# Two graph layers on one core: gather offsets read from resident tables, block numbers loaded quad by quad

## The chip, the core and the metric

The kernel runs on one core of one Trainium2 chip, in one launch. The metric is the device time of that launch in microseconds. An engine is named as the profile names it: PE (TensorE, with PEld for its weight loads), DVE (VectorE), ACT (ScalarE), POOL (GpSimd) and SP (SyncE, which issues DMAs here). Each has its own instruction queue, and semaphores order the queues against each other.

## The reference

Two attention layers over one graph of 6250 nodes and 106250 edges (50000 pairs in both directions and a loop at each node), the edges sorted by destination. Width 128; the first layer has 8 heads, the second 4. Shortened:

```python
# layer 0
Q, K, V = x @ Wq, x @ Wk, x @ Wv                       # [n, 8, 16]
q_dst = Q[dst] + rel_q[type2]
k_src = K[src] + rel_k[type2] + time_emb @ Wt + bt
v_src = V[src] + rel_v[type2]
euclid = sum(q_dst * k_src) / sqrt(16) * decay          # decay: a small MLP of edge time and type
hyp    = -beta * norm(m[src] - m[dst]) * decay          # m: x mapped into the ball
logits = alpha * euclid + (1 - alpha) * hyp
ex     = exp(logits - segment_max(logits, dst)[dst])
agg    = segment_sum(v_src * ex / denom[dst], dst)
x = layernorm(x + block(x, agg))                        # Wo, two norms, an FFN with gelu
# layer 1
logits = sum(leaky_relu(xs[src] + xd[dst] + edge_emb[type8], 0.2) * att)
agg    = segment_sum(xs[src] * softmax_by_dst(logits), dst)
x = layernorm(x + film_norm(x, agg))
```

## The kernel before

`front` prepares: node tables in DRAM, index tables, the decay of each edge. `edges0` is the first pass over the edges (first layer), then `join_tiles` and `nodes0` finish that layer; `edges1` is the second pass, then `join_tiles` and `nodes1`. The change touches `edges0` and `edges1` alone.

The sorted edges are cut into 831 tiles of 128. The nodes are cut into 53 blocks of 120. A *step* is one tile against one block, so that a tile whose destinations cross a border has two steps; the steps are padded to 896. Four steps are a *quad*, and 221 quads are worked in each pass, one after the other, all written out (`whole(emit)`). Each engine runs its own list `emit(None, c)` for c = 0, 1, ...

**POOL** gathers the rows of the source nodes. `gather(i, c)` issues four indirect DMAs for quad c, each of 128 rows with 128 offsets, one a partition, into a ring of 12 quads in the first pass (`RQ0`) and 16 in the second (`RQ`). Before the four it waits for `sums`: PE must be done with the quad that held this place of the ring. In the kernel before it also waits, once in a group of quads (4 in the first pass, 8 in the second), for `idx_in`. The offsets for all steps lie in one resident table, `k.index0` in the first pass (128 x 896 integers) and `index1` in the second (brought in by a DMA at its start). ACT copies the 16 or 32 columns of one group from it into a small buffer `idx` (three buffers, or two), and the gather reads its offsets from there. ACT's copy itself waits until the rows of an older group have landed (`index`, L1217 and L1936).

**PE** forms, for each quad of the first pass, the time term (L1298), differences and query products by an identity and a transposed one-hot matmul (L1306, L1308), and seven to eight quads later the sums per destination (L1320).

**DVE** does the rest of the first pass in the order of `emit` (L1120): the key addition L1146 (waits for the rows of the quad), the product L1151 (waits for PE's points), the reduction L1156, the transposed one-hot L1117, the one-hot comparison L1164 for the quad 7 back, the scaling of values L1180, and between these four additions `add(0)` to `add(3)` (L1135). Each addition takes one step's result, two more quads back (a = c - 9), and adds it to the block of the accumulator whose number stands in the table `tile_block`. That number must be in a register of DVE's queue before the instruction is issued. `load_steps` (L944) brings numbers there: one load of up to sixteen. Once in four quads there is extra work: L1169 and L1183 in one quad, L1174, L1188, L1195 and L1199 in the next.

Before the change, DVE loads the numbers of four quads at the head of a quad:

```python
if live(i, a) and (a % 4 == 3 or a == 0):
    count["blocks"] = load_steps(nc, k, ET.DVE, 1, nth0(i, a, QS), 4 if a % 4 == 3 else 3)
```

The quad before has ended with a wait for its last addition (L1201) and a count of the semaphore `added` (L1202).

**ACT** copies the sums out of PSUM (L1252), squares differences (L1260) and issues DMAs; **SP** issues the other loads.

The second pass has the same order of things with fewer operations: L1867, L1872, L1876, L1883, L1886, four additions L1896 and the one-hot L1854 on DVE. Its block numbers are loaded by the same helper between L1886 and the additions, those of four quads at a time (of one quad the first time); that is not changed.

Of the kernel before, what the change touches and what calls it, by code (L numbers as in the profile page):

```python
# [20 lines left out]
I32 = mybir.dt.int32  # L21
# [3 lines left out]
ET = mybir.EngineType  # L25

P = 128
# [933 lines left out]
def edges0(nc, k):  # L961
# [7 lines left out]
    with ExitStack() as ctx:  # L969
# [6 lines left out]
        feat = [sb(f"feat{u}", [P, P]) for u in range(6)]  # L976
        idx = [sb(f"idx{u}", [P, GS], I32) for u in range(3)]
        oht = [sb(f"oht{u}", [P, QS * P]) for u in range(3)]
# [17 lines left out]

        weights_in, ready, idx_in = sem("weights_in"), sem("ready"), sem("idx_in")
        node_in, group_in, bound_out = ([sem(f"{m}{u}") for u in range(3)] for m in ("node_in", "group_in", "bound_out"))
# [10 lines left out]
        def live(i, c):  # L1009
            return i is not None or 0 <= c < sz.quads  # L1010
# [13 lines left out]
        with nc.Block() as block:  # L1024
# [60 lines left out]
            @block.gpsimd  # L1085
            def _(pl):
                def gather(i, c):
                    if c % LQ0 == 0:
                        pl.wait_ge(idx_in, group(i, c, 1, 1))
                    if i is not None or c >= RQ0:  # L1090
                        pl.wait_ge(sums, nth0(i, c - RQ0 + 1, 2))
                    apart(pl, k.passed)
                    for t in range(QS):
                        nc.gpsimd.indirect_dma_start(  # L1094
                            rows[:, c % RQ0 * QS + t, 0:3 * D], None, k.d_table0,
                            bass.IndirectOffsetOnAxis(ap=idx[c // LQ0 % 3][:, c % LQ0 * QS + t:c % LQ0 * QS + t + 1], axis=0))\
                            .then_inc(rows_in[c % RQ0], 16)

                for c in range(sz.quads):
                    gather(None, c)  # L1100

            @block.vector
            def _(dve):
# [16 lines left out]
                def emit(i, c):  # L1120
# [3 lines left out]
                    key = rows[:, r:r + QS, 0:D]  # L1124
                    if live(i, a) and (a % 4 == 3 or a == 0):
                        count["blocks"] = load_steps(nc, k, ET.DVE, 1, nth0(i, a, QS), 4 if a % 4 == 3 else 3)

                    def add(t):
                        if not live(i, a):
                            return  # L1130
                        if t == 0:
                            dve.wait_ge(evicted, nth0(i, a + 1, 2))
                        to = acc[:, bass.ds(count["blocks"][((a - 3) % 4 if a >= 3 else a) * QS + t], 1), :]
                        dve.wait_ge(vec, count["added"])
                        v.did(V.tensor_tensor(to, to, bound[a // BQ % 3][0:BN, a % BQ * QS + t, :].unsqueeze(1), ALU.add))  # L1135
                        count["added"] = v.base + v.n
# [24 lines left out]
                    if live(i, w):  # L1161
                        if i is not None or w >= 2:
                            dve.wait_ge(sums, nth0(i, w - 1, 2))
                        V.tensor_tensor(oh[w % 2][:, :, :], bc(k.iota[:, 0:R_LAST + 1], 1, QS),  # L1164
                                        bc(k.code[:, bass.ds(nth0(i, w, QS), QS)], 2, R_LAST + 1), ALU.is_equal)
                    if leveling:
                        u = m // LQ0 % 3
                        dve.wait_ge(rooted, group(i, m, 1, 1))
                        v.did(V.tensor_tensor(far[:, :, :], bc(k.heads[:, 1, :], 2, GS), bc(dist[:, :], 1, H0), ALU.mult))  # L1169
# [30 lines left out]
                    if live(i, a):  # L1200
                        dve.wait_ge(vec, count["added"])  # L1201
                        dve.sem_inc(added, 1)  # L1202
                    count["base"] += v.n

# [9 lines left out]
            def _(act):  # L1214
                A = nc.scalar

                def index(i, c):  # L1217
                    if i is not None or c >= 3 * LQ0:
                        b = c - 2 * LQ0 - 1
                        act.wait_ge(rows_in[b % RQ0], slot(i, b, RQ0, 16 * QS))  # L1220
                    A.copy(idx[c // LQ0 % 3][:, :], k.index0[:, bass.ds(nth0(i, c, QS), GS)]).then_inc(idx_in, 1)

# [13 lines left out]
                def emit(i, c):  # L1236
                    w, m1 = c - LAG0 - 1, c - 3 - LQ0
                    if c % LQ0 == 1 and live(i, c - 1 + 2 * LQ0):
                        index(i, c - 1 + 2 * LQ0)
                    if c % LQ0 == 3 and live(i, m1):  # L1240
# [36 lines left out]

                for g in range(2):
                    index(None, g * LQ0)
                for c in range(5):  # L1280
# [459 lines left out]
def edges1(nc, k):  # L1740
# [5 lines left out]
    with ExitStack() as ctx:  # L1746
# [8 lines left out]
        att = sb("att", [P, D])  # L1755
        idx = [sb(f"idx{u}", [P, LQ * QS], I32) for u in range(2)]
        oht = [sb(f"oht{u}", [P, QS * P]) for u in range(4)]
# [13 lines left out]
        att_in, index_in = sem("att_in"), sem("index_in")  # L1771
        idx_in, node_in = sem("idx_in"), [sem(f"node_in{u}") for u in range(2)]
        gate_in = [sem(f"gate_in{u}") for u in range(2)]
# [15 lines left out]
        with nc.Block() as block:  # L1789
# [29 lines left out]
            @block.gpsimd  # L1819
            def _(pl):  # L1820
                def gather(i, c):
                    if c % LQ == 0:
                        pl.wait_ge(idx_in, c // LQ + 1 if i is None else i * 2 + (c // LQ + 1))
                    if i is not None or c >= RQ:
                        pl.wait_ge(sums, nth(i, c - RQ + 1, 2))
                    apart(pl, k.passed)
                    for t in range(QS):
                        r = c % RQ * QS + t
                        nc.gpsimd.indirect_dma_start(  # L1829
                            rows[:, r, :], None, k.d_table1,  # L1830
                            bass.IndirectOffsetOnAxis(ap=idx[c // LQ % 2][:, c % LQ * QS + t:c % LQ * QS + t + 1], axis=0))\
                            .then_inc(rows_in[c % RQ], 16)

                for c in range(sz.quads):
                    gather(None, c)
# [97 lines left out]
            def _(act):  # L1933
                A = nc.scalar

                def index(i, c):  # L1936
                    u = c // LQ % 2
                    if i is not None or c >= 2 * LQ:
                        b = c - LQ - 1
                        act.wait_ge(rows_in[b % RQ], 16 * QS * (b // RQ + 1) if i is None else i * (16 * QS) + 16 * QS * (b // RQ + 1))  # L1940
                    A.copy(idx[u][:, :], index1[:, bass.ds(nth(i, c, QS), LQ * QS)]).then_inc(idx_in, 1)  # L1941

                def emit(i, c):
                    w, m = c - LAG, c - LQ
                    if c % LQ == 2 and live(i, c - 2 + LQ):
                        index(i, c - 2 + LQ)
                    if c % LQ == 1 and live(i, c - 1 - LQ):
# [25 lines left out]

                act.wait_ge(index_in, 16)
                index(None, 0)
                whole(emit)
# [506 lines left out]
```

## Time and profile before

| what | us |
|---|---|
| the three timed runs | 3217.82, 3219.7, 3222.8 |
| their median | 3219.7 |
| span of the profiled execution, first to last instruction | 3217.7 |
| mean granted TensorE clock over the span | 0.893 of full speed |

| engine | busy us | share |
|---|---|---|
| PE | 2416.1 | 75% |
| PEld | 1874.0 | 58% |
| DVE | 2465.3 | 77% |
| ACT | 1142.9 | 36% |
| POOL | 1955.3 | 61% |

The profiled span is 2.0 us under the median and 0.1 us under the fastest run. An operation is named by the line of the code and the tiles that it writes and reads; buffer numbers are left out, so `pair<-d_table,e_idx` is a gather from the node table, with offsets in `idx`, into the ring of rows that lives in `pair`. "Idle before" is the time that the engine stood before an instruction, and the name behind the arrow what ended it; "issue" means that nothing in the profile was waited for. Register loads are instructions of an engine's queue and not counted as busy. The gathers of the first pass start between 304.0 and 1473.8 us, those of the second between 1870.7 and 3024.9 us.

### The profile page before, as it was taken

What the parts mean: (1) busy time and instruction counts of PE and PEld (TensorE: products, weight loads), DVE (VectorE), ACT (ScalarE), POOL (GpSimd) and SP (SyncE); (2) the same over time, 40 slices, a digit from 0 to 9 for tenths busy, and PEclk for the clock granted to TensorE, in tenths of its full rate; (3) what the DMA queues carried; (4) which work ended last, traced back from release to release, by engine and by line L of the source; (5) the groups of instructions that cost most, each with busy time, mean ns of one, the idle gap of its engine ahead of it and who ended that gap; (6) DMA issues with size and microseconds to landing.
All of it is one profiled execution on the core that took longest, in us unless ns stands there. A gap on an engine that the chain in (4) does not pass through costs nothing. (4 is left out here: it accounts for less than half of the span.)

```text
span 3217.7 us, 48588 instructions
## 1 busy us (share of the span) xinstructions
PE 2416.1 (75%) x11946; PEld 1874.0 (58%) x11946; DVE 2465.3 (77%) x5962; ACT 1142.9 (36%) x3885; POOL 1955.3 (61%) x1957
## 2 busy tenths in 40 slices
PE   4895888988888888896688847666776666666644
PEld 3664666666666666665333436555666666665533
DVE  7444898898988898888566647877777777777868
ACT  2442455555555555553255501111111111111206
POOL 1001777777777777774500057777777777777464
PEclk9797999999999999997799977989888888888865
DMA  5387766666666666663000133333333333333131
GB/s 112 62 228 209 204 194 194 193 196 196 191 191 192 195 193 196 193 193 111 21 19 25 32 91 82 82 81 81 75 77 79 82 81 82 82 81 81 35 61 41
DMA packets 253626, 387.12 MB, mean 120 GB/s; under 512 B 70853, under 2 KB 168881, under 8 KB 249642
## 3 DMA queue, kind: packets, MB, share of 16 engines
q0 software_dynamic: 86432, 239.62, 27.8%
q1 hardware_dynamic: 132662, 130.96, 16.2%
q10 hardware_dynamic: 34260, 13.43, 1.7%
q8 instruction: 107, 1.75, 0.2%
q14 instruction: 165, 1.35, 0.1%
HBM read 342.88 MB, written 40.92 MB: 119 GB/s over the span
## 5 line engine op out<-in xcount | busy, mean ns | idle before, releaser
L1829 POOL DMA_INDIRECT pair<-d_table,e_idx x884 | 886.0, 1002 | 569.0 <-ACT e_idx L1941 299.9
L1094 POOL DMA_INDIRECT pair<-d_table,e_idx x884 | 901.6, 1020 | 276.5 <-issue 252.4
L1993 PE MATMUL e_p_x<-pair,iden 128*128 128x264 f32 x884 | 340.8, 473 | 313.4 <-issue 211.2
L1960 ACT COPY pair<-e_p_r 122x264 f32<-122x264 f32 x442 | 167.3, 378 | 860.9 <-PE e_p_r L2019 837.7
L1308 PE MATMUL e_p_x<-big,e_oht 128*128 x1768 | 454.8, 380 | 0.0
L1308 PEld LDWEIGHTS e_p_x<-big,e_oht 128*128 128x128 f32 x1768 | 336.9, 191 | 46.2
L1993 PEld LDWEIGHTS e_p_x<-pair,iden 128*128 128x128 f32 x884 | 160.6, 226 | 343.3 <-issue 283.5
L1995 PEld LDWEIGHTS e_p_x<-big,e_oht 128*128 128x128 f32 x1768 | 327.5, 229 | 45.6
L1298 PE MATMUL e_p_t<-e_wbd,e_feat 128*128 128x512 f32 x442 | 243.6, 633 | 145.2 <-DVE pair L1146 117.4
L2019 PE MATMUL e_p_r<-pair,e_oh 128*122 128x132 f32 x1768 | 278.9, 307 | 77.9 <-DVE pair L1883 77.6
L1995 PE MATMUL e_p_x<-big,e_oht 128*128 x1768 | 325.3, 315 | 0.0
L2019 PEld LDWEIGHTS e_p_r<-pair,e_oh 128*122 128x122 f32 x1768 | 249.1, 210 | 97.7 <-DVE pair L1883 97.1
L1867 DVE SCALAR_TENSOR_TENSOR e_prod<-e_p_x,e_att 128x512 f32<-128x512 f32 x221 | 151.2, 684 | 197.2 <-PE e_p_x L1995 196.6
L1260 ACT ACTIVATE e_p_x<-e_p_x 128x128 f32<-128x128 f32 x884 | 234.4, 265 | 180.2 <-DVE pair L1151 179.3
L1135 DVE TENSOR_TENSOR big<-big,e_bound 120x136 f32 x884 | 258.0, 292 | 22.7 <-DVE e_lg L1183 15.0
L1306 PE MATMUL e_p_x<-pair,iden 128*128 128x256 f32 x884 | 264.3, 381 | 0.4 <-issue 0.3
L1320 PE MATMUL e_p_r<-pair,e_oh 128*122 128x136 f32 x1768 | 253.1, 287 | 7.2 <-DVE pair L1180 7.2
L1320 PEld LDWEIGHTS e_p_r<-pair,e_oh 128*122 128x122 f32 x1768 | 228.1, 189 | 28.4 <-DVE pair L1180 21.4
L1306 PEld LDWEIGHTS e_p_x<-pair,iden 128*128 128x128 f32 x884 | 168.6, 191 | 119.5 <-issue 107.5
L1896 DVE TENSOR_TENSOR big<-big,pair 120x132 f32 x884 | 212.6, 292 | 32.3 <-issue 19.0
L1146 DVE TENSOR_TENSOR pair<-pair,e_p_t 128x512 f32<-128x512 f32 x221 | 151.5, 686 | 97.5 <-issue 72.6
L1252 ACT COPY e_bound<-e_p_r 122x272 f32<-122x272 f32 x442 | 164.3, 384 | 142.5 <-PE e_p_r L1320 65.3
(359 smaller groups left out, 4012.9 us busy)
## 6 DMA issues: line engine op xcount, KB each, us to landing
pair<-d_table,e_idx POOLq DMA_INDIRECT x1768, 2.5
e_node<-d_node SPq DMA_DIRECT2D x28, 960.0 KB
e_node<-d_node SPq DMA_DIRECT2D x111, 240.0 KB
d_table<-tab_kmv SPq DMA_DIRECT2D x54, 360.0 KB
e_feat<-in_edge_attr ACTq DMA_DIRECT2D x442, 16.0 KB
e_feat<-in_edge_attr SPq DMA_DIRECT2D x442, 16.0 KB
e_gate<-d_gate SPq DMA_DIRECT2D x84, 64.5 KB
d_decay<-pair SPq DMA_DIRECT2D x7, 512.0 KB, 4.0
```

Source lines behind the costliest of these rows:

```text
L1094: nc.gpsimd.indirect_dma_start(rows[:, c % RQ0 * QS + t, 0:3 * D], None, k.d_table0, bass.IndirectOffsetOnAxis(ap=idx[c // LQ0 % 3][:, c % ...
L1135: v.did(V.tensor_tensor(to, to, bound[a // BQ % 3][0:BN, a % BQ * QS + t, :].unsqueeze(1), ALU.add))
L1260: last = A.activation(p_x[c % 2][:, t, D:2 * D], p_x[c % 2][:, t, D:2 * D], ACT.Square, accum_out=d2[c // LQ0 % 3][:, c % LQ0 * QS + t:c % ...
L1298: M(p_t[:, :, :].rearrange("p t d -> p (t d)"), feat[c % 6][:, :], wbd[:, :, :].rearrange("p t d -> p (t d)"), start=True, stop=True).then ...
L1306: M(x[:, 2 * h:2 * h + 2, D:2 * D], k.iden[:, :], rows[:, r + 2 * h:r + 2 * h + 2, D:2 * D], start=True, stop=True)
L1308: last = M(x[:, t, :], oht[c % 3][:, t * P:(t + 1) * P], qm[:, bass.ds(of[t], 1), :], start=False, stop=True, skip_group_check=True)
L1320: last = M(p_r[h][0:R_LAST + 1, t - 2 * h, 0:W], oh[w % 2][:, t, :], rows[:, w % RQ0 * QS + t, 2 * D:R0], start=True, stop=True)
L1829: nc.gpsimd.indirect_dma_start(rows[:, r, :], None, k.d_table1, bass.IndirectOffsetOnAxis(ap=idx[c // LQ % 2][:, c % LQ * QS + t:c % LQ * ...
L1896: v.did(V.tensor_tensor(to, to, bound[a // 4 % 2][0:BN, a % 4 * QS + t, :].unsqueeze(1), ALU.add))
L1993: M(x[:, 2 * h:2 * h + 2, 0:W], k.iden[:, :], rows[:, r + 2 * h:r + 2 * h + 2, :], start=True, stop=False)
L1995: last = M(x[:, t, 0:W], oht[c % 4][:, t * P:(t + 1) * P], xd[:, bass.ds(held["blocks"][(c - 1) % 4 * QS + t if c else t], 1), :], start=F ...
L2019: last = M(p_r[h][0:R_LAST + 1, t - 2 * h, 0:W], oh[w % 2][:, t, :], rows[:, w % RQ * QS + t, :], start=True, stop=True)
```

## The change

In both passes the buffers `idx`, ACT's copies into them (`index` and its calls), the semaphore `idx_in` and POOL's wait for it are gone. A gather names its 128 offsets in the resident table itself. In the second pass POOL waits once, before its first gather, for the DMA that brings the table. In the first pass DVE no longer loads the block numbers of four quads at the head of a quad; in each quad it loads the four numbers of the next quad's additions, behind the one-hot comparison and ahead of the scaling.

```diff
@@ edges0, POOL
                 def gather(i, c):
-                    if c % LQ0 == 0:
-                        pl.wait_ge(idx_in, group(i, c, 1, 1))
                     if i is not None or c >= RQ0:
                         pl.wait_ge(sums, nth0(i, c - RQ0 + 1, 2))
...
-                            bass.IndirectOffsetOnAxis(ap=idx[c // LQ0 % 3][:, c % LQ0 * QS + t:c % LQ0 * QS + t + 1], axis=0))\
+                            bass.IndirectOffsetOnAxis(ap=k.index0[:, c * QS + t:c * QS + t + 1], axis=0))\
@@ edges0, DVE
-                    if live(i, a) and (a % 4 == 3 or a == 0):
-                        count["blocks"] = load_steps(nc, k, ET.DVE, 1, nth0(i, a, QS), 4 if a % 4 == 3 else 3)
-
...
-                        to = acc[:, bass.ds(count["blocks"][((a - 3) % 4 if a >= 3 else a) * QS + t], 1), :]
+                        to = acc[:, bass.ds(count["blocks"][t], 1), :]
...
                                         bc(k.code[:, bass.ds(nth0(i, w, QS), QS)], 2, R_LAST + 1), ALU.is_equal)
+                    if live(i, a + 1):
+                        upcoming = load_steps(nc, k, ET.DVE, 1, nth0(i, a + 1, QS), 1)
...
                         dve.sem_inc(added, 1)
+                    if live(i, a + 1):
+                        count["blocks"] = upcoming
@@ edges0, ACT
-                def index(i, c):
-                    if i is not None or c >= 3 * LQ0:
-                        b = c - 2 * LQ0 - 1
-                        act.wait_ge(rows_in[b % RQ0], slot(i, b, RQ0, 16 * QS))
-                    A.copy(idx[c // LQ0 % 3][:, :], k.index0[:, bass.ds(nth0(i, c, QS), GS)]).then_inc(idx_in, 1)
...
-                    if c % LQ0 == 1 and live(i, c - 1 + 2 * LQ0):
-                        index(i, c - 1 + 2 * LQ0)
...
-                for g in range(2):
-                    index(None, g * LQ0)
@@ edges1, POOL
-                    if c % LQ == 0:
-                        pl.wait_ge(idx_in, c // LQ + 1 if i is None else i * 2 + (c // LQ + 1))
...
-                            bass.IndirectOffsetOnAxis(ap=idx[c // LQ % 2][:, c % LQ * QS + t:c % LQ * QS + t + 1], axis=0))\
+                            bass.IndirectOffsetOnAxis(ap=index1[:, c * QS + t:c * QS + t + 1], axis=0))\
...
+                pl.wait_ge(index_in, 16)
                 for c in range(sz.quads):
                     gather(None, c)
@@ edges1, ACT: index(i, c), its two calls and the wait for index_in are gone in the same way
```

## Rows read from the trace of the kernel before

**Rows 1.** Waits of DVE, 400 to 1450 us: waiter, releaser, total us, times, longest.

```profile
DVE pair L1146 <- issue: 67.5, 50, 1.4
DVE pair L1146 <- DVE big L1135: 23.0, 99, 0.6
```

**Rows 2.** Page, costliest groups: busy, mean ns; idle before and releasers.

```profile
L1829 POOL DMA_INDIRECT pair<-d_table,e_idx x884 | 886.0, 1002 | 569.0 <-ACT e_idx L1941 299.9
L1306 PE MATMUL e_p_x<-pair,iden 128*128 128x256 f32 x884 | 264.3, 381 | 0.4 <-issue 0.3
```

**Rows 3.** Timeline of DVE, first pass: start, us, operation, idle before it.

```profile
1037.52 0.69 DVE L1146 TENSOR_TENSOR pair<-pair,e_p_t 128x512 f32<-128x512 f32 x1 [1.36 <-issue]
...
1040.97 0.28 DVE L1169 TENSOR_TENSOR e_far<-heads,e_dist 128x128 f32<-128x128 f32 x1
...
1042.32 0.30 DVE L1135 TENSOR_TENSOR big<-big,e_bound 120x136 f32 x1 [0.27 <-DVE e_lg L1183]
...
1052.51 0.29 DVE L1135 TENSOR_TENSOR big<-big,e_bound 120x136 f32 x1
1053.01 0.69 DVE L1146 TENSOR_TENSOR pair<-pair,e_p_t 128x512 f32<-128x512 f32 x1 [0.21 <-DVE big L1135]
...
1055.62 0.30 DVE L1135 TENSOR_TENSOR big<-big,e_bound 120x136 f32 x1
1055.83 0.66 DVE L1164 TENSOR_TENSOR e_oh<-iota_f,code 128x488 f32<-128x488 f32 x1
1056.41 0.69 DVE L1180 TENSOR_TENSOR pair<-pair 128x512 f32<-128x512 f32 x1
1057.01 0.29 DVE L1135 TENSOR_TENSOR big<-big,e_bound 120x136 f32 x1
1058.67 0.69 DVE L1146 TENSOR_TENSOR pair<-pair,e_p_t 128x512 f32<-128x512 f32 x1 [1.36 <-issue]
```

**Rows 4.** The gathers of the first pass (L1094): durations, ends of POOL's idle time.

```profile
L1094 POOL DMA_INDIRECT pair<-d_table,e_idx x884: 942/946/2656, 304.0 to 1473.8; - x177
  issue: 252.4, 828
  ACT e_idx L1221: 7.6, 2
```

**Rows 5.** Busy time (x instructions) of the engines in a stretch of each pass.

```profile
400.00:1450.00 1050.00, 938.57 (x4464) 720.67 (x4463) 942.24 (x2281) 562.79 (x2327) 808.74 (x791) 1.00 0.68 194
2000.00:3000.00 1000.00, 684.07 (x3889) 603.69 (x3888) 774.26 (x1993) 166.32 (x480) 766.11 (x768) 0.86 0.34 80
```

**Rows 6.** Timeline of POOL, first pass, same four quads.

```profile
1041.05 1.01 POOL L1094 DMA_INDIRECT pair<-d_table,e_idx  x1 [0.30 <-issue]
1042.37 1.06 POOL L1094 DMA_INDIRECT pair<-d_table,e_idx  x1 [0.30 <-issue]
...
1052.54 1.08 POOL L1094 DMA_INDIRECT pair<-d_table,e_idx  x1 [0.30 <-issue]
...
1056.42 1.71 POOL L1094 DMA_INDIRECT pair<-d_table,e_idx  x1 [0.30 <-issue]
```

**Rows 7.** Timeline of ACT at the start of the first pass.

```profile
303.02 0.31 ACT L1221 COPY e_idx<-index 128x16 int32<-128x16 int32 x2 [11.78 <-PEq L908]
```

**Rows 8.** Loads of block numbers on DVE's queue (L949): ns least/median/most.

```profile
L949 DVEq TENSOR_LOAD <-tile_block x112: 343/1099/1115, 364.5 to 3053.3; - x112
```

**Rows 9.** Waits of DVE, 2000 to 3000 us.

```profile
DVE e_prod L1867 <- PE e_p_x L1995: 154.3, 50, 8.4
DVE big L1896 <- issue: 17.0, 24, 1.0
```

**Rows 10.** Timeline of DVE, first quads of the second pass.

```profile
1946.38 0.95 DVE L1896 TENSOR_TENSOR big<-big,pair 120x132 f32 x4
```

**Rows 11.** Groups by line, DVE, second pass.

```profile
L1883 DVE TENSOR_TENSOR pair<-pair 128x512 f32<-128x512 f32 x221 | 150.3, 680 | 0.0
L1872 DVE TENSOR_TENSOR e_oh<-iota_f,code 128x488 f32<-128x488 f32 x221 | 145.2, 657 | 1.3
```

More of the change, by code:

```diff
@@ L976, in edges0 @@
         feat = [sb(f"feat{u}", [P, P]) for u in range(6)]
-        idx = [sb(f"idx{u}", [P, GS], I32) for u in range(3)]
         oht = [sb(f"oht{u}", [P, QS * P]) for u in range(3)]
@@ L995, in edges0 @@
         p_l, p_e = p_le[:, 0:P], p_le[:, 2 * P:3 * P]
-        weights_in, ready, idx_in = sem("weights_in"), sem("ready"), sem("idx_in")
+        weights_in, ready = sem("weights_in"), sem("ready")
         node_in, group_in, bound_out = ([sem(f"{m}{u}") for u in range(3)] for m in ("node_in", "group_in", "bound_out"))
@@ L1755, in edges1 @@
         att = sb("att", [P, D])
-        idx = [sb(f"idx{u}", [P, LQ * QS], I32) for u in range(2)]
         oht = [sb(f"oht{u}", [P, QS * P]) for u in range(4)]
@@ L1771, in edges1 @@
         att_in, index_in = sem("att_in"), sem("index_in")
-        idx_in, node_in = sem("idx_in"), [sem(f"node_in{u}") for u in range(2)]
+        node_in = [sem(f"node_in{u}") for u in range(2)]
         gate_in = [sem(f"gate_in{u}") for u in range(2)]
@@ L1934, in _ @@
                 A = nc.scalar
[L1936 to L1941, printed above, removed]
                 def emit(i, c):
                     w, m = c - LAG, c - LQ
-                    if c % LQ == 2 and live(i, c - 2 + LQ):
-                        index(i, c - 2 + LQ)
                     if c % LQ == 1 and live(i, c - 1 - LQ):
@@ L1972, in emit @@
                                top[m // LQ % 2][:, 0:P:P - 1].unsqueeze(1)).then_inc(kept, 1)
-                act.wait_ge(index_in, 16)
-                index(None, 0)
                 whole(emit)
```

## The prediction

> **What bounds the kernel now.** I read the busy shares first, then the two gather lines, then the waits of DVE and POOL inside each edge pass, then single instructions. No engine is busy over 77% of the span, so the shares alone name no bound. The two passes over the edges take most of it: the gathers of the first run from 304 to 1475 us, those of the second from 1871 to 3026 us, and both parts of the change lie there.
>
> In the first pass DVE waits for no other engine and for no row. Between 400 and 1450 us its idle time is its own: 67.5 us in 50 stops before the key addition at L1146 (1.35 us each, "issue") and 23.0 us in 99 short stops before the same line [rows 1]. PE hardly stops before the matmul L1306 that reads the gathered rows (0.4 us in all) [rows 2]. So rows arrive in time, and DVE's own queue sets the pace. The 1.35 us stop stands once in four quads, right where the sixteen block numbers are loaded: behind the last addition of a quad 0.21 us pass in an ordinary quad (1052.51 + 0.29 to 1053.01) and 1.36 us in a loading one (1057.01 + 0.29 to 1058.67) [rows 3].
>
> POOL is not idle either. Its idle time before a gather is 252.4 us in 828 pieces of 0.30 us, a fixed gap; a gather takes 0.946 us in the median, so back to back one needs 1.25 us [rows 4]. Yet 791 of them take 1050 us, 1.327 us each, and in the second pass 768 take 1000 us, 1.302 us each [rows 5]. The surplus sits in lengthened gathers, and the trace shows what lengthens them: the gather that starts at 1056.42 ends at 1058.13, 0.83 us after DVE's L1135 (which follows L1180 without a break) ends at 1057.30. The one at 1052.54 ends 0.82 us after an L1135, that at 1042.37 0.81 us after another, that at 1041.05 0.81 us after L1169 [rows 3, 6]. All these have two inputs in SBUF: a gather that meets such an operation waits until it ends. The first pass is therefore held from two sides: DVE paces it, and POOL, with no rest, would run only little faster.
>
> That is the rule of the Trainium skill, SBUF — State Buffer, section "SBUF: two separate sides": the port pair of VectorE and GpSimd is an exclusive lock, against a GpSimd instruction that reads SBUF also for a VectorE operation with two SBUF inputs, and the other side stands still. The trace agrees (the 0.81 to 0.83 us above). It speaks against this change: time freed on DVE is not time freed on the port. By it alone, with as much waiting per gather as now, the gain is nil, which is the second rival below.
>
> **The change part by part.** *Offsets straight from the tables.* Removed: 56 copies on ACT in the first pass (one in four quads), 28 in the second, ACT's wait for older rows ahead of each, and POOL's wait for the copy. ACT is busy for 0.54 of the first pass and 0.17 of the second [rows 5], so its relief is worth nothing. The wait for a copy ended idle time of POOL twice in the first pass, 7.6 us in all, and once in the second [rows 2, 4]; that one of 299.9 us is the node stage between the passes, which stays. What becomes late next is the wait for sums in the ring, which POOL has now as well. The gather itself is the same instruction with 128 offsets from another address; bounds: the least gather took 0.942 us and the median one 0.946 [rows 4], so plus or minus 0.004 us times 1768, 7 us either way; I take 0, the shape of the read being the same. The first gather of each pass no longer waits for a copy and its semaphore: 0.5 us each, an estimate between nothing and the 1 us from the first copy (303.0) to the first gather (304.0) [rows 4, 7]. Sum: 1 us less for the two passes.
>
> *Block numbers.* Removed: a load of sixteen, 1.10 us on DVE's queue, every four quads; added: a load of four each quad, 0.34 us, the smallest duration on that line, which is the first load of the second pass [rows 8]. It stands behind the one-hot comparison L1164. Is it hidden there? The second pass has its loads behind queued work already, one of sixteen in four quads: some 48 in the 1000 us stretch, 1.10 us each, would be 53 us if bare, and "issue" before the additions there is 17.0 us [rows 9]. Its first load, the one of four, left no gap before the additions at 1946.38 [rows 10]. In its new place the load comes after 0.66 us of comparison has been queued, and moves past the key addition, the product and three of the four additions, none of which waits for it any more; behind it are L1180 and the last addition. A load of 0.34 us under 0.66 us costs nothing. If that cover fails, four loads are 1.37 us a cycle of four quads, more than the 1.15 us that they free; L1180, the last addition, PE's sums, and POOL's ring that waits for those, are then late by it.
>
> The skill's DMA: Bandwidth & Descriptors, section "Latency and other measured facts", gives a floor of about 600 ns for such a load and says that loads are grouped to spread it, which argues against splitting. The 0.34 us here is under that floor, so the measurement decides. By the page, with the cover gone, four loads would be 2.4 us a cycle, and the change some 66 us slower (1.25 x 53, an estimate).
>
> So on DVE a cycle of four quads loses 1.36 - 0.21 = 1.15 us, some 53 times: 61 us. This is the most that the first pass can give.
>
> *What is late next: POOL.* A cycle takes 21.14 us now (1037.52 to 1058.67), and DVE alone would need 20.0 [rows 3]. POOL needs 16 x 1.25 = 20.0 without a single wait. A wait-free cycle isn't to be had: L1135, L1164, L1180 and L1135 hold the port without a break from 1055.7 to 1057.3, 1.6 us, longer than the 1.25 us between gathers, so one is caught in every such stretch. So POOL becomes the bound, DVE will wait for rows, and the question is how long a gather then waits on average. The nearest row is the second pass, where POOL is the bound today and DVE waits 154.3 us for PE [rows 9]: 1.302 us a gather, 0.052 over the floor. The first pass holds the port a little longer per quad: four additions of 0.29, L1164 and L1180, and a quarter of three 0.28 us operations, 2.7 us [rows 3], against 2.5 in the second (four additions of 0.29, L1872, L1883) [rows 11]; 0.052 x 1.07 = 0.056, so 1.306 us. Against 1.327 that is 0.021 us on some 840 gathers (those after DVE's additions have begun): 18 us. Bounds: 0.077 x 840 = 65 us if no gather waited (DVE then stops it at 61), and a loss as in the third rival. I take 18.
>
> **Sum.** 18 + 1 = 19 us off the profiled 3217.7, so 3198.7; the median of the runs is 2.0 above that span, so I forecast 3201 us. Likeliest case's own range: 3190 to 3213.
>
> **Rivals.**
> 1. *DVE keeps the pace* and all of the stop is won: 3219.7 - 62 = 3158 us. For it: no wait of DVE on rows now. Against it: POOL would need cycles of 20.0, without the waits just shown. Chance 0.10.
> 2. *The port hides it*: gathers wait as much as now, 1.17 us a cycle over the floor, whoever is the bound. Then DVE's 1.15 us turn into a wait for rows before L1151 or L1146; time 3214 to 3226, say 3219. For it: POOL shows no rest now. Chance 0.22. That the removed copies do nothing is part of this and of the forecast alike.
> 3. *Slower: the caught gather.* Today one gather in a cycle pays the long wait, 0.76 us (1.71 - 0.95); in the other three stretches of held port a gather pays 0.06 to 0.13 [rows 6]. That is an alignment which DVE's own pace keeps up: its stop of 1.36 us comes after the stretch, and the port is free there. If DVE follows the landing of rows instead, each stretch falls at a place fixed to the gathers, and a second stretch may pay too: 0.65 us more a cycle, 53 cycles, 34 us, hence 3254 us. It decides when more than 1.17 us of waiting come together in a cycle. For it: the stretch of 1.6 us exceeds the gathers' spacing, and the free 1.15 us vanish. Against it: the second pass, which runs that way, waits less. Chance 0.28, of which 0.04 for bare loads (4 x 0.34 - 1.15 = 0.22 us a cycle: 12 us slower).
>
> **How the numbers follow.** The forecast has 0.40, the rivals 0.10, 0.22 and 0.28. A run of this kernel tells 0.2% (6.4 us) from no change. Faster: 0.40 + 0.10 = 0.50; same 0.22; slower 0.28. The range goes from 3163, which leaves out most of the first rival, to 3250, which leaves out about a third of the last: 3163 to 3250, some 0.17 outside. Both signs are inside since what a gather waits at the port can't be read from a trace in which DVE runs at another rhythm.
>
> **What would show it.** Right: no stop of 1.36 us before L1146; loads of 0.34 us, 221 of them, with no new idle time before L1180; waits of DVE or PE on rows in the first pass, which there are none of now; gathers at 1.30 to 1.31 us each between 400 and 1400 us; the second pass as before. Wrong: idle time before L1180 (the loads are bare); a cycle of 20.0 us with DVE still without waits (the port gave way); more than 1.33 us a gather (the third rival); a second pass that moves by more than 5 us (the offsets' place matters after all).

## The result: slower by 0.75%

The changed kernel takes 3248.31 us (median of five runs, 3240.09 to 3256.23), the kernel before 3219.7 in the runs beside it (3215.82 to 3234.64): the recorded ratio over the runs is 1.0075, interval 1.0055 to 1.0094 (the two medians by themselves give 1.0089). The profiled run took 3245.12 us, its span is 3243.3. From its first gather to the end of its last the first pass grew from 1170.7 to 1200.9 us. The second went from 1155.1 to 1148.8, within what it varies by in all runs below (1145 to 1159). The front before the first gather grew by 9.6 us and the stretch between the passes shrank by 9.5; in all runs below the first gather starts between 304 and 327 us, and the kernel before has the earliest.

The waits of DVE in the first pass, 400 to 1450 us of the changed kernel (waiter, releaser, total us, times, longest), against [rows 1]:

```profile
DVE pair L1145 <- PE e_p_x L1296: 76.7, 71, 3.8
DVE pair L1140 <- DVE big L1129: 30.9, 143, 0.2
...
DVE pair L1140 <- issue: 0.8, 3, 0.3
```

The stop is gone, 67.5 us became 0.8. In its place DVE's product waits 76.7 us for PE, and PE for the rows: before the matmul that reads them it is idle 136.4 us, where it was 0.4 [rows 2]. Some of these waits stand under the name of the transposed one-hot (second line, PE's waits from 400 to 1450 us). That name is of a later quad: in all 63 of them the one-hot that PE needed had ended at least 4.5 us earlier, and PE starts 2.1 to 4.4 us after the quad's last gather ends on POOL.

```profile
L1294 PE MATMUL e_p_x<-pair,iden 128*128 128x256 f32 x884 | 280.8, 400 | 136.4 <-issue 77.1
...
PE e_p_x L1294 <- DVE e_oht L1114: 55.0, 63, 1.9
```

The loads by line and engine queue (least, median, most ns) and the gathers of the first pass, against [rows 8, 4]. A load of four takes 0.347 us, there are 221 of them beside the second pass's 56, and DVE's waits show no new idle time at L1176 behind them.

```profile
L949 DVEq TENSOR_LOAD <-tile_block x277: 341/347/1108, 373.1 to 3079.8; - x139
```

```profile
L1091 POOL DMA_INDIRECT pair<-d_table,index x884: 942/949/2652, 313.6 to 1513.5; - x177
```

Busy time and instructions of PE, PEld, DVE, ACT and POOL in a stretch of each pass, then the granted TensorE clock, the DMA engines' busy share and GB/s, against [rows 5]:

```profile
400.00:1450.00 1050.00, 910.86 (x4352) 698.59 (x4351) 923.58 (x2226) 542.56 (x2223) 815.30 (x771) 0.99 0.67 189
2000.00:3000.00 1000.00, 681.81 (x3921) 600.57 (x3921) 782.13 (x2012) 162.56 (x460) 764.43 (x774) 0.87 0.37 81
```

The first pass completes 771 gathers where it completed 791: 1.362 us each instead of 1.327. The gap between gathers is still 0.30 us; the gathers themselves are longer. Over all 884, what exceeds 0.945 us sums to 96.3 us, before 66.2: that difference of 30.1 us is the pass's 30.2.

What lengthens them shows in the timelines (start, us, idle before in brackets) of POOL and of DVE in the changed kernel:

```profile
846.19 2.03 POOL L1091 DMA_INDIRECT pair<-d_table,index  x1 [0.30 <-issue]
...
869.49 1.90 POOL L1091 DMA_INDIRECT pair<-d_table,index  x1 [0.30 <-issue]
```

```profile
845.73 0.66 DVE L1158 TENSOR_TENSOR e_oh<-iota_f,code 128x488 f32<-128x488 f32 x1
846.31 0.28 DVE L1165 TENSOR_TENSOR e_far<-heads,e_dist 128x128 f32<-128x128 f32 x1
846.51 0.69 DVE L1176 TENSOR_TENSOR pair<-pair 128x512 f32<-128x512 f32 x1
847.11 0.28 DVE L1179 TENSOR_TENSOR e_lg<-e_lg,e_far 128x128 f32<-128x128 f32 x1
847.66 0.30 DVE L1129 TENSOR_TENSOR big<-big,e_bound 120x136 f32 x1 [0.27 <-DVE e_lg L1179]
848.18 0.69 DVE L1140 TENSOR_TENSOR pair<-pair,e_p_t 128x512 f32<-128x512 f32 x1 [0.22 <-DVE big L1129]
...
852.20 0.69 DVE L1145 TENSOR_TENSOR pair<-pair,e_p_x 128x512 f32<-128x512 f32 x1 [3.12 <-PE e_p_x L1296]
...
870.28 0.28 DVE L1179 TENSOR_TENSOR e_lg<-e_lg,e_far 128x128 f32<-128x128 f32 x1
```

The gather of 846.19 begins inside the run from L1158 to L1179 and ends at 848.22, 0.83 us after L1179 ends (847.39); that of 869.49 ends 0.83 us after the next L1179 (870.56). DVE then stands 3.12 us for rows. Counted so between 400 and 1450 us (gathers lengthened by more than 0.08 us that end 0.78 to 0.87 us after a DVE operation): before, 148 gathers caught up to an addition, 0.36 us each on average, made 53.6 of the stretch's 61 us; now it is 87 us, of which 30 gathers are caught up to L1179 for 1.01 us each, 46 up to an addition for 0.41 and 100 up to L1176 for 0.20.

### The profile page after: what moved, and what is told of

Same layout as the page of the kernel before. It is cut to its first block and busy times, and to the rows that moved or that the text cites. A ratio compares the mean times of both kernels' runs of the same rounds, so it can differ in the third digit from the quotient of the medians.

```text
span 3243.3 us, 48669 instructions
## 1 busy us (share of the span) xinstructions
PE 2410.6 (74%) x11946; PEld 1869.8 (58%) x11946; DVE 2469.1 (76%) x5962; ACT 1131.1 (35%) x3801; POOL 1979.3 (61%) x1957
## 3 DMA queue, kind: packets, MB, share of 16 engines
q8 instruction: 107, 1.75, 0.2%
## 5 line engine op out<-in xcount | busy, mean ns | idle before, releaser
L1814 POOL DMA_INDIRECT pair<-d_table,pair x884 | 879.8, 995 | 563.2 <-DMA pair<-d_index 294.1
L1091 POOL DMA_INDIRECT pair<-d_table,index x884 | 931.7, 1054 | 276.5 <-issue 260.9
L1296 PE MATMUL e_p_x<-big,e_oht 128*128 x1768 | 466.2, 387 | 0.0
L1294 PE MATMUL e_p_x<-pair,iden 128*128 128x256 f32 x884 | 280.8, 400 | 136.4 <-issue 77.1
L1296 PEld LDWEIGHTS e_p_x<-big,e_oht 128*128 128x128 f32 x1768 | 344.8, 195 | 49.7
L1968 PEld LDWEIGHTS e_p_x<-pair,iden 128*128 128x128 f32 x884 | 160.1, 225 | 339.1 <-issue 261.8
L1970 PEld LDWEIGHTS e_p_x<-big,e_oht 128*128 128x128 f32 x1768 | 327.4, 229 | 45.6
L1994 PE MATMUL e_p_r<-pair,e_oh 128*122 128x132 f32 x1768 | 272.1, 302 | 83.2 <-DVE pair L1869 82.9
L1294 PEld LDWEIGHTS e_p_x<-pair,iden 128*128 128x128 f32 x884 | 159.3, 194 | 301.0 <-issue 173.1
L1970 PE MATMUL e_p_x<-big,e_oht 128*128 x1768 | 325.6, 315 | 0.0
L1286 PE MATMUL e_p_t<-e_wbd,e_feat 128*128 128x512 f32 x442 | 231.9, 606 | 44.7 <-DMA e_feat<-in_edge_attr 25.2
L1145 DVE TENSOR_TENSOR pair<-pair,e_p_x 128x512 f32<-128x512 f32 x221 | 151.0, 683 | 92.3 <-PE e_p_x L1296 91.5
```

What stands on the lines that cost most here:

```text
L1091: nc.gpsimd.indirect_dma_start(rows[:, c % RQ0 * QS + t, 0:3 * D], None, k.d_table0, bass.IndirectOffsetOnAxis(ap=k.index0[:, c * QS + t:c ...
L1286: M(p_t[:, :, :].rearrange("p t d -> p (t d)"), feat[c % 6][:, :], wbd[:, :, :].rearrange("p t d -> p (t d)"), start=True, stop=True).then ...
L1294: M(x[:, 2 * h:2 * h + 2, D:2 * D], k.iden[:, :], rows[:, r + 2 * h:r + 2 * h + 2, D:2 * D], start=True, stop=True)
L1296: last = M(x[:, t, :], oht[c % 3][:, t * P:(t + 1) * P], qm[:, bass.ds(of[t], 1), :], start=False, stop=True, skip_group_check=True)
L1814: nc.gpsimd.indirect_dma_start(rows[:, r, :], None, k.d_table1, bass.IndirectOffsetOnAxis(ap=index1[:, c * QS + t:c * QS + t + 1], axis=0))\
L1968: M(x[:, 2 * h:2 * h + 2, 0:W], k.iden[:, :], rows[:, r + 2 * h:r + 2 * h + 2, :], start=True, stop=False)
```

## The experiments

Three numbers are taken from each profiled trace: the *lengthening* (durations of the first pass's 884 gathers less 0.945 us each), the mean *cycle* (every 16 gathers, one cycle of four quads, 55 in a run) and how many are *steady* (21.10 to 21.20 us). Ratios are to the kernel before, run beside it on the same chip. A trace is of one execution, which is not always a typical one (e2's took 3283.6 us against a median of 3259.7, g2's 3216.6 against 3225.5), so the last three columns carry the scatter of single executions, and the ratio decides.

| kernel | ratio [interval] | lengthening | cycle | steady |
|---|---|---|---|---|
| before | 1 | 66.2 | 21.20 | 40 |
| changed | 1.0075 [1.0055, 1.0094] | 96.3 | 21.74 | 2 |
| e1_offsets | 0.9997 [0.9981, 1.0012] | 74.2 | 21.35 | 22 |
| e2_numbers | 1.0063 [1.0044, 1.0082] | 128.2 | 22.29 | 2 |
| e3_stop16 | 1.0062 [1.0039, 1.0085] | 104.9 | 21.90 | 0 |
| e4_apart | 0.9944 [0.9923, 0.9965] | 65.6 | 21.19 | 8 |
| f1_stop10 | 1.0130 [1.0109, 1.0152] | 121.3 | 22.20 | 0 |
| f2_stop2 | 1.0154 [1.0132, 1.0176] | 117.5 | 22.13 | 1 |
| f3_four | 1.0113 [1.0094, 1.0131] | 102.3 | 21.85 | 2 |
| f4_apart_four | 1.0082 [1.0064, 1.0100] | 96.5 | 21.74 | 1 |
| g1_const | 1.0066 [1.0046, 1.0085] | 97.5 | 21.77 | 0 |
| g2_used | 1.0004 [0.9990, 1.0019] | 63.3 | 21.15 | 43 |
| g3_hid16 | 1.0080 [1.0055, 1.0105] | 95.5 | 21.73 | 3 |
| g4_apart_before | 0.9971 [0.9955, 0.9986] | 54.7 | 20.99 | 10 |
| h1_stop9 | 1.0053 [1.0034, 1.0072] | 93.5 | 21.70 | 2 |
| h2_stop8 | 1.0075 [1.0049, 1.0101] | 92.4 | 21.67 | 2 |
| h3_stop7 | 1.0093 [1.0071, 1.0116] | 100.3 | 21.82 | 0 |
| k1_stop9_late | 1.0105 [1.0082, 1.0128] | 118.6 | 22.14 | 0 |
| k2_stop10_late | 1.0140 [1.0117, 1.0163] | 122.4 | 22.21 | 2 |

**The theories.** A: the old stop made DVE the slower side and held its port-holding operations at a fixed place beside the gathers; without it DVE follows the rows and catches more gathers. B: reading the offsets from the large table is slower. C: the 221 loads disturb. F came later: only a stop in which DVE is idle keeps the place.

**Which part costs.** e1 takes only the offsets, e2 only the loads of four (the copies stay).

```
e1:  to = acc[:, bass.ds(count["blocks"][((a - 3) % 4 ...) * QS + t], 1), :]   # and the load of 16 as before
e2:  ap=idx[c // LQ0 % 3][...]                                       # copies and waits as before
```

> Only the offsets come straight from the tables; block numbers are loaded for four quads as before. Theory A (lost step: without its stop of 1.36 us a cycle, DVE is no longer the slower side, POOL sets the pace, and gathers meet the stretches of DVE operations with two SBUF inputs at a worse place): DVE keeps its stop, so the first pass is as before, 21.14 us a cycle of four quads, and the time 3215 to 3225 us. Theory B (a gather that reads its offsets from the big table is slower): all of the loss is here, about 3245 us, with gathers longer than 0.946 us in the median. Theory C (the 221 loads disturb DVE or the port): as A here.

> Only the block numbers are loaded quad by quad behind the one-hot comparison; the copies of offsets stay. A: all of the loss is here, 3238 to 3256 us, gathers of the first pass at about 1.36 us each, DVE waiting for PE before its product. B: 3215 to 3225 us. C: as A here.

e1 is no change, e2 has the loss: B falls, and the removed copies were worth nothing, as predicted. (In its one trace e1's first pass takes 1178.8 us, 8 more than before, and keeps the steady cycle for 22 of 55.) The cause is A or C.

**Stop or loads.** e3 was to put the old stop back by a load of 16 whose numbers nobody uses.

```
+ if live(i, a) and (a % 4 == 3 or a == 0):
+     load_steps(nc, k, ET.DVE, 1, nth0(i, a, QS), 4 if a % 4 == 3 else 3)
```

> The changed kernel with one more load of sixteen numbers, which nothing uses, at the head of every fourth quad, where it was before: work is added, and with it the stop of DVE comes back. A: the loss goes, 3215 to 3225 us, cycles of 21.14 us. B: stays at 3248 us or above. C: the 221 loads of four are still there, so 3248 us or above.

It tells nothing: its trace has 277 loads on DVE's queue and no stop, as in the changed kernel.

```profile
L949 DVEq TENSOR_LOAD <-tile_block x277: 342/347/1105, 370.0 to 3092.4; - x139
```

The unused load is not among them (g2 below, with both, has 333), so the run repeats the changed kernel. The test was made again with the numbers in use (g2), with no load at all (g1), and with a quarter of the loads (g3). g1 leaves out the block numbers: its additions, as many and as long, go to blocks fixed in advance, so its sums land in the wrong blocks.

```
g1:  to = acc[:, c % 3 * QS + t:c % 3 * QS + t + 1, :]          # no load of block numbers
g2:  + if live(i, a) and (a % 4 == 3 or a == 0): count["sixteen"] = load_steps(... 16 or 12 numbers)
     bass.ds((count["blocks"] if t % 2 else count["sixteen"][((a - 3) % 4 ...) * QS:])[t], 1)
g3:  if live(i, a + 1) and ((a + 1) % 4 == 3 or a + 1 == 0): upcoming = load_steps(... 16 or 12 numbers)
```

> The changed kernel without any load of block numbers in the first pass: the additions go to blocks that are fixed when the program is built (c % 3 * 4 + t), as many and as long as before, so the sums land in the wrong blocks; neither the old stop nor the 221 loads are there. Theory A (without the stop VectorE is no longer the slower side and follows the landing of the rows, where its held stretches catch more gathers): the loss is there without any load, ratio to the kernel before 1.005 to 1.008, gathers lengthened by 90 to 105 us in sum, irregular cycles. Theory C (the 221 loads disturb): the loss goes and the stop's time is won as well, ratio 0.985 to 0.999.

> The changed kernel with both: the load of 16 numbers and its stop at the head of every fourth quad as before, whose numbers serve additions 0 and 2, and the 221 hidden loads of 4, whose numbers serve additions 1 and 3; the result is the same. Theory A: with the stop back the loss goes, ratio 0.998 to 1.002, runs of cycles of 21.1 us, gathers lengthened by 65 to 75 us. Theory C: with the 221 loads still there the loss stays, 1.006 or more.

> The changed kernel with its hidden load made for four quads at a time: 16 numbers behind the comparison of every fourth quad, 56 loads instead of 221, and no stop. Theory A: the loss stays as in the changed kernel, 1.005 to 1.008. Theory C: a quarter of the loads, so a quarter of the loss and the stop won: 0.990 to 1.001.

All three ratios came out as A said (g2's lengthening of 63.3 lies just under A's 65 to 75). Without any load the loss is there, and with the stop back it is gone although the loads of four stay. The waits of DVE and the first pass's stretch, g1 first, then g2:

```profile
DVE pair L1145 <- PE e_p_x L1292: 80.3, 82, 3.5
...
400.00:1450.00 1050.00, 903.72 (x4337) 695.12 (x4336) 925.00 (x2221) 543.82 (x2220) 815.52 (x770) 0.99 0.67 188
```

```profile
DVE pair L1143 <- issue: 68.1, 51, 1.7
...
400.00:1450.00 1050.00, 939.20 (x4466) 721.63 (x4465) 942.98 (x2282) 553.53 (x2285) 808.34 (x794) 1.00 0.69 194
```

In g2 DVE stands still for 68.1 us in its stops, and yet 794 gathers go through instead of 770. A steady cycle of g2 on POOL: one gather of sixteen is caught for 0.76 us, and its like 21.14 us later for the same.

```profile
554.87 1.71 POOL L1091 DMA_INDIRECT pair<-d_table,index  x1 [0.30 <-issue]
...
576.01 1.70 POOL L1091 DMA_INDIRECT pair<-d_table,index  x1 [0.30 <-issue]
```

**Held stretches set apart.** e4 reorders DVE's operations in the changed kernel so that no more than two or three with two inputs in SBUF follow each other, g4 does so in the kernel before.

```
before: key add, add0, product, add1, reduction, transposed one-hot, add2, comparison, far|scaled_l, scaling, ..., add3
e4, g4: key add, add0, product, add1, comparison, reduction, add2, scaling, far|scaled_l, transposed one-hot, ..., add3
```

> The changed kernel with DVE's operations of a quad in another order: the comparison stands ahead of the reduction, the scaling ahead of the transposed one-hot, so that the longest unbroken run of operations with two SBUF inputs falls from 1.6 us to 0.8 (1.0 in one quad of four). Work and loads are the same. A: no stretch is longer than the 1.25 us between gathers, their waiting falls below the 1.17 us a cycle of the kernel before, the first pass to 20.3 to 20.9 us a cycle, and the time to 3180 to 3210 us, faster than both kernels. B and C: the order costs or gives nothing, 3240 to 3256 us.

> The kernel before (old loads with their stop, copies of the offsets) with the new order of VectorE's operations alone, which in the changed kernel gave 0.9944. Theory A: with held stretches short it matters little who is slower; the stop adds its 1.36 us a cycle to VectorE, whose work fills 20 us of the 21.1, so 0.997 to 1.003. Theory C: the order's gain without the loads' loss, 0.986 to 0.990.

e4 is faster than before by 0.56% and, by its ratio against the changed kernel's, by 1.3% than that: the change is no loss in this order. g4's 0.29% shows that the order alone wins something. Whether removing the stop adds to it is open, as the two intervals overlap and the one profile of each points the other way (lengthening 65.6 and 54.7). g4 has a steady cycle of its own, 23 of its 55 at 20.95 to 21.05 us. In e4 DVE's product still waits for PE, as in the changed kernel, though less:

```profile
DVE pair L1145 <- PE e_p_x L1296: 57.8, 62, 3.7
```

What follows the comparison decides how long a gather caught in it waits. In all traces together 466 caught gathers begin 0.05 to 0.45 us into the comparison of 0.66 us. Where the reduction (e4, g4) or the operation with an input in PSUM (L1170 of the changed kernel) follows, all 182 wait to the comparison's end only, 0.28 us on average; where another operation with two inputs in SBUF follows, 144 of 284 wait to the end of the whole run, and the average of the 284 is 0.63 us.

f3 and f4 take the comparison's second SBUF input away, by four tensor_scalar operations, in the changed kernel and in e4's order.

```
- V.tensor_tensor(oh[w % 2][:, :, :], bc(k.iota...), bc(k.code...), ALU.is_equal)
+ for t in range(QS):
+     V.tensor_scalar(oh[w % 2][:, t, :], k.iota[:, 0:R_LAST + 1], k.code[:, bass.ds(nth0(i, w, QS, t), 1)], None, ALU.is_equal)
```

> The changed kernel with the one-hot comparison (two inputs from SBUF, 0.66 us, port held) written as four tensor_scalar comparisons, one per step of the quad (one input from SBUF and a scalar per partition), same result. Theory A: a held stretch of 0.66 us per quad is gone, gathers are lengthened by 60 to 75 us instead of 96, ratio 0.996 to 1.001. Theory C: the loss stays at 1.006 or 1.007, since the loads are as they were.

> The reordered kernel that was 0.56% faster than before (held operations set apart by others) with the comparison as four tensor_scalar operations as well. Theory A: fewer held stretches, each of one operation: gathers lengthened by 40 to 55 us instead of 66, ratio 0.986 to 0.991. If the gathers wait no less for it (some other limit of POOL or the landing sets the pace): 0.994 as without it.

Both missed: gathers lengthened by more than 0.3 us rose from 89 to 146 in f3. That is not for want of a free port in these operations: in f4 88 gathers begin within 0.55 us of the first of the four, and none is lengthened by more than 0.09 us, while in e4 all 62 that begin 0.08 to 0.45 us into the single comparison are caught, for 0.29 us on average. The gathers are caught elsewhere: in f3 134 begin in the first 0.45 us of the scaling and wait 0.58 us each (in the changed kernel 116, for 0.23), in f4 75 in the transposed one-hot (0.08 to 0.30 us in) for 0.42. The four take 0.86 us together against 0.66 for the one, so DVE also has more to do; what of the loss is that, these runs don't separate.

**A stop made of work.** Can any delay of DVE stand in for the old stop? f1, h1, h2 and h3 put an unused reduction at its place, 10, 9, 8 or 7 times 122 columns (1.42, 1.30, 1.17 and 1.04 us); f2 spreads it over all quads; k1 and k2 delay DVE by a further 4.3 us once, early in the pass.

```
+ if live(i, a) and a % 4 == 3:                       # f2: every a, n = 2
+     V.tensor_reduce(spare[:, 0:n], bc(k.iota[:, 0:R_LAST + 1], 1, n), AX.X, ALU.add)
k1, k2: + if a == 2: two such reductions of 16 x 122
```

> The changed kernel with one VectorE reduction of 122 columns taken ten times (1,220 elements, one input from SBUF, the result unused) at the head of every fourth quad of the first pass, where the load of 16 numbers stood; by the row of the reduction of 512 (0.68 us) it should last some 1.33 us, as long as the old stop of 1.36 us. The loads of four stay. Theory A (the stop kept VectorE's held stretches of the port at a fixed place beside the gathers; without it they drift onto the gathers): the loss goes, ratio to the kernel before 0.998 to 1.002, cycles of four quads steady at 21.1 us, gathers lengthened by 66 us in sum. Theory C (the 221 loads themselves disturb): the loss stays, 1.006 or 1.007, with 96 us or more.

> The same with the reduction cut to 2 x 122 columns (some 0.32 us) at the head of every quad, so that VectorE's work in a cycle of four quads is as long as before (4 x 0.32 = 1.27 us) but without the one long gap. Theory A in the form 'only VectorE's total work in a cycle counts': ratio 0.998 to 1.002. Theory A in the form 'the one long gap in a cycle, and where it falls, is what counts': 1.003 to 1.007, with irregular cycles. Theory C: 1.006 or 1.007.

> The changed kernel with the unused reduction at the head of every fourth quad cut from 10 to 9 times 122 columns: by the difference of a tenth (1.42 us for ten) some 1.30 us, and from the end of the last addition to the key addition 1.32 us, as with the old stop, where ten gave 1.45 us. Theory A with the phase as its core (after the old stop the first gather of the next cycle begins 0.2 us ahead of the key addition, and the gather of the next long held stretch then begins just as the comparison ends; ten times made it begin 0.1 us too early, and it was caught for 0.95 us more): the steady cycle of 21.1 us is back, ratio to the kernel before 0.998 to 1.003, gathers lengthened by 65 to 75 us. Rival theory F (a stop filled with work on VectorE never restores it, only an idle VectorE does): 1.010 or more as with ten.

> The same with 8 times 122 columns, some 1.17 us. Theory A: VectorE's cycle is 0.13 us shorter than with the old stop, and the gathers can follow it if the phase allows: 0.995 to 1.001 with a steady cycle of about 21.0 us, or, if the steady state is not reached, 1.004 to 1.010. Theory F: 1.010 or more.

> The same with 7 times 122 columns, some 1.04 us. Theory A: VectorE's cycle is some 20.8 us; the stop is now shorter than one gather with its gap (1.25 us), so I expect no steady state: 1.004 to 1.008, close to the changed kernel. If it is steady: 0.990 to 0.996. Theory F: between 1.0075 (no stop) and 1.013 (ten).

> The kernel with the reduction of 9 times 122 columns at the head of every fourth quad, and once, at the third quad with additions, two more unused reductions of 16 times 122 columns (about 2.2 us each, 4.4 us in all), so that VectorE enters the pass 4.4 us further behind the gathers. Without them this kernel ran the steady cycle of 21.14 us at first (from 448 to 491 us) and left it when its product waited 0.23 us for PE. Theory A with a margin (the steady cycle lives as long as VectorE never waits for rows, so the distance by which it trails the gathers keeps it): the steady cycle holds for most of the pass, gathers lengthened by 63 to 75 us, ratio 0.998 to 1.003, better by 0.3 to 0.7% than without the two (1.0053). Theory F (a stop in which VectorE works cannot hold it): 1.005 to 1.010, 4 us of delay on top at most.

> The same delay with the reduction of 10 times 122 columns, where VectorE's cycle is 0.13 us longer than the steady one. Theory A with a margin: VectorE can pace the gathers at 21.27 us if a steady cycle exists at that length: ratio 1.001 to 1.005; if none exists there (the phase fits 21.14 only), as without the delay, 1.010 to 1.015. Theory F: 1.010 to 1.015.

None brought the loss to nothing. A's numbers for f1, f2, h1, h3 and k1 were wrong (h3 by little: 1.0093 against 1.004 to 1.008); F is right that no filled stop makes the loss go, but not in its sizes (h1 and h2 are below its 1.010, k1 just over its 1.005 to 1.010). The filling itself catches no gather: of 135 that begin 0.08 to 0.80 us into the reduction in f1, the three h and the two k runs none is lengthened by more than 0.03 us. Neither the length of the stop alone nor the distance by which DVE trails the gathers makes the steady cycle last. The traces show how narrow that cycle is. h1 does run it, with the gathers at the same places to 0.02 us as in g2, from 448.5 to 485.3 us. Then its product waits for PE, the comparison comes 0.3 us later against the gathers, and the gather of 488.77 is let in at the comparison's end, lengthened by 0.24 us, where its like was held through scaling and addition for 0.75 (DVE and POOL of h1):

```profile
486.46 0.69 DVE L1149 TENSOR_TENSOR pair<-pair,e_p_x 128x512 f32<-128x512 f32 x1 [0.23 <-PE e_p_x L1300]
...
488.48 0.66 DVE L1162 TENSOR_TENSOR e_oh<-iota_f,code 128x488 f32<-128x488 f32 x1
```

```profile
488.77 1.18 POOL L1092 DMA_INDIRECT pair<-d_table,index  x1 [0.30 <-issue]
```

k1 trails by more and still misses it, by some 10 ns. In g2 a gather begins 0.06 us after the transposed one-hot and goes free, while that operation takes 0.52 us; in k1 it begins 0.07 us after, is caught for 0.28 us, and the operation takes 0.48 (g2, then k1; DVE, then POOL):

```profile
559.33 0.52 DVE L1114 TENSOR_SCALAR e_oht<-e_node,part 128x512 f32<-128x512 bf16 x1
...
559.39 0.95 POOL L1091 DMA_INDIRECT pair<-d_table,index  x1 [0.30 <-issue]
```

```profile
418.02 0.48 DVE L1115 TENSOR_SCALAR e_oht<-e_node,part 128x512 f32<-128x512 bf16 x1
...
418.09 1.23 POOL L1092 DMA_INDIRECT pair<-d_table,index  x1 [0.30 <-issue]
```

The other traces confirm the edge: of the first-pass gathers of all 19 that begin 0 to 0.055 us after this operation's start none of 115 is lengthened by more than 0.03 us, of those 0.075 to 0.30 us after it all 839 are, and between the two 71 of 202. So a filled stop of the same length may land DVE on the wrong side of an edge of 0.02 us. That this is why the filled stops fail is read from traces, not tested by a run. What makes the idle stop land on the right one in before, e1 (in 22 of 55 cycles) and g2 stays open.

## Why the prediction was wrong

- *Offsets at nothing*: right. e1 is 0.9997; its second pass took 1151.3 us.
- *The load of four hidden, the stop gone*: right. 0.347 us, no idle time behind it; g1, without loads, costs the same as the changed kernel.
- *DVE's cycle*: right in size. Four quads without a wait take 5.27 + 5.56 + 4.50 + 4.51 = 19.84 us in the changed kernel; I had 20.0. POOL's floor is 16 x 1.2475 = 19.96 (0.9425 and 0.305).
- *POOL becomes the bound, DVE waits for rows*: right, 76.7 us of it.
- *"The nearest row is the second pass... so 1.306 us"*: this is the step that failed. Measured: 1.362 us, 0.035 more than before instead of 0.021 less; on 840 gathers 29 us lost where I had 18 won. The forecast took the waiting of a gather from the time for which DVE holds the port in a quad (0.052 x 1.07), as if the place of these stretches beside the gathers did not matter; only rival 3 let the waiting grow. Nor were the 1.327 us before what POOL needed: they were nearly all what DVE allowed. DVE's own cycle with the stop is 19.84 + 1.15 = 20.99 us (g4's steady cycle), POOL's floor 19.96. In the steady 21.14 us POOL's gathers wait 1.14 us, and that they wait costs only the 0.15 us by which this exceeds 20.99. (That floor and waits add up to the cycle proves nothing: POOL stands still for nothing but its 0.30 us gaps.) Once DVE's cycle is below POOL's, every caught microsecond is on the path, and without the fixed place there are more: 96.3 us over the pass's 55 cycles, 1.75 a cycle. I had also missed that DVE itself is held up: in the kernel before its transposed one-hot takes 0.48 us in most quads, but in one of the steady cycle

```profile
1050.56 0.65 DVE L1117 TENSOR_SCALAR e_oht<-e_node,part 128x512 f32<-128x512 bf16 x1
```

- The second pass was a poor neighbour: other operations, in another order, decide where gathers are caught. e4 shows how much the order is worth without the stop, 1.3%.
- *Rival 3, the caught gather*: what happened. Its size was 0.65 us on 53 cycles, 34 us; the pass lost 30.2. Its condition, more than 1.17 us of waiting in a cycle, was met. Its picture was too orderly: the second stretch does not pay at a fixed place in each cycle, the cycles wander from 20.7 to 23.8 us once the additions run, so that its size came so close is partly luck.
- *Rival 2, the port hides it*, had the right reason (time freed on DVE is not time freed on the port) and a floor where there is none: without the stop the port takes more than it did. The rule of the Trainium skill, SBUF — State Buffer, section "SBUF: two separate sides", which I weighed beside it, is borne out again by 0.83 us from L1179's end to that of the gather caught in front of it.

## What to carry to other kernels

An idle stop on the engine that sets the pace can be what pays for the other engines' waits: before it is removed, add up what the next engine needs per cycle with its waits in, not its floor, and ask whether those waits shrink or grow when nobody waits for it any more. Where VectorE and GpSimd share a port, spread VectorE's two-input operations before taking time off VectorE. And look in the trace whether an experiment's added work is really there.

## What the hardware showed that I had not expected

- Two engines whose own cycles are 19.96 us (POOL) and 20.99 (DVE with its stop) lock to a common one in which the faster one's waits fill the difference: 43 cycles of 55 at 21.10 to 21.20 us in g2, and 2 in the changed kernel.
- A gather that begins up to 0.055 us after the transposed one-hot is free, and one that begins 0.075 us after it is caught, in the example above for 0.28 us.
- A gather holds VectorE up as well: in the first passes of all traces the 647 transposed one-hots that start 0.48 to 0.70 us after the start of an unlengthened gather take 0.55 to 0.71 us, the 1189 that start 0.05 to 0.40 us after one take 0.47 to 0.49.
- The key addition and the product, with one of two inputs in PSUM, caught none of the 2729 gathers that begin 0.08 to 0.40 us into them.
- Reductions with one input in SBUF (L1150) ended the waiting of no gather where I counted; the transposed one-hot (L1114), one input too but in bf16, does, by 0.13 us for 49 gathers of the changed kernel.
- The loss follows the length of a filled stop without order: 1.04, 1.17, 1.30 and 1.42 us gave 1.0093, 1.0075, 1.0053 and 1.0130.
